# Attention in a transformer layer: softmax weights left unnormalised, row sums from a column of ones, division after the context's reload

## The reference

```python
q, k, v = (split_heads(x @ w + b) for w, b in ((wq, bq), (wk, bk), (wv, bv)))
scores = einsum('bhqd,bhkd->bhqk', q, k) * 48 ** -0.5 + attn_bias[:, None]
attn = softmax(scores, axis=-1)
ctx = einsum('bhij,bhjd->bhid', attn, v)          # back to (b, n, 384)
x1 = rmsnorm(x + ctx @ wo + bo, alpha1, gamma1)
x2 = rmsnorm(x1 + silu(x1 @ w1 + b1) @ w2 + b2, alpha2, gamma2)
out = layernorm(x + x2)
```

## Time and profile before

| | us |
|---|---|
| median of 3 runs | 2019.77 |
| lowest, highest | 2019.53, 2022.11 |
| profiled execution, its own time | 2022.79 |
| its span, first to last instruction | 2021.0 |
| busy: PE, PEld, DVE, ACT, POOL | 1951.2, 1696.9, 1457.0, 1231.1, 1007.5 |
| mean granted TensorE clock | 0.990 |

### The profile page before, as it was taken

The page is one execution under the profiler, slowest core; times in us unless marked ns, Lnnn a source line. Parts: engine busy times, 40 slices in busy tenths (PEclk is TensorE's granted clock), DMA queues, the critical chain, the costliest instruction groups (busy, mean ns, idle before and its releaser), DMA issues. The chain is left out here.

```text
span 2021.0 us, 37267 instructions
## 1 busy us (share of the span) xinstructions
PE 1951.2 (97%) x10336; PEld 1696.9 (84%) x10336; DVE 1457.0 (72%) x3022; ACT 1231.1 (61%) x2408; POOL 1007.5 (50%) x1005
## 2 busy tenths in 40 slices
PE   6999999999999999999996999999999999999998
PEld 5887878888788878888775899999999999999997
DVE  5898899888898898988994555655555555555644
ACT  4887788877887788878874444444433443444332
POOL 3444444443444444443453666555556665555643
PEclk8999999999999999999997999999999999999999
DMA  6444544456444544456434222222111222222011
GB/s 204 117 125 121 164 125 128 125 139 164 110 124 125 159 130 134 119 137 164 111 89 157 83 75 78 78 78 78 66 55 43 72 76 78 78 78 78 16 40 39
DMA packets 114581, 210.12 MB, mean 104 GB/s; under 512 B 18160, under 2 KB 46576, under 8 KB 114544
## 3 DMA queue, kind: packets, MB, share of 16 engines
q1 hardware_dynamic: 114544, 209.67, 35.6%
HBM read 96.35 MB, written 37.75 MB: 66 GB/s over the span
## 5 line engine op out<-in xcount | busy, mean ns | idle before, releaser
L376 POOL TENSOR_SCALAR probs<-probs,inv_sum 128x512 f32<-128x512 f32 x256 | 401.9, 1570 | 515.7 <-DVE inv_sum L545 514.2
L444 ACT ACTIVATE probs<-probs,neg_max 128x512 f32<-128x512 f32 x512 | 364.6, 715 | 79.6 <-DVE neg_max L539 79.1
L531 DVE CUSTOM_DVE_ANT_0 probs<-ps_s,adj_s 128x512 f32<-128x512 f32 x480 | 309.6, 681 | 46.1 <-DMA adj_s<-in_adj 42.2
L557 DVE TENSOR_TENSOR pT_lo<-ps_t,pT_hi 128x1024 fp32r<-128x1024 f32 x256 | 312.0, 1219 | 27.5 <-ACT pT_hi L452 26.7
L452 ACT ACTIVATE pT_hi<-ps_t 128x1024 fp32r<-128x1024 f32 x256 | 261.4, 1021 | 88.7 <-PE ps_t L674 86.5
L1132 DVE TENSOR_TENSOR h_lo<-hidden,h_hi 128x512 fp32r<-128x512 f32 x192 | 168.5, 879 | 172.5 <-ACT h_hi L1038 172.0
L674 PEld LDWEIGHTS ps_t<-ident,probs 128*128 128x128 f32 x2048 | 240.2, 141 | 36.3 <-DVE probs L551 2.4
L674 PE MATMUL ps_t<-ident,probs 128*128 128x128 f32 x2048 | 266.8, 273 | 1.5 <-DVE probs L551 1.5
L1247 PE MATMUL ps_y<-w_hi,h_hi 128*128 128x384 f32 x768 | 257.9, 336 | 0.0
L1247 PE MATMUL ps_y<-w_hi,h_lo 128*128 128x384 f32 x768 | 256.6, 334 | 0.0
L1247 PE MATMUL ps_y<-w_lo,h_hi 128*128 128x384 f32 x768 | 256.6, 334 | 0.0
(11 more groups left out here) (104 smaller groups left out, 4071.4 us busy)
## 6 DMA issues: line engine op xcount, KB each, us to landing
q_both<-stage_q SPq DMA_DIRECT2D x192, 192.0 KB, 3.7
ctx_dram<-ctx_stage SPq DMA_DIRECT2D x256, 96.0 KB, 2.0
k_hl<-stage_k SPq DMA_DIRECT2D x192, 96.0 KB, 2.4
adj_s<-in_adj SPq DMA_DIRECT2D x32, 512.0 KB, 3.9
xT_raw<-in_xT SPq DMA_DIRECT2D x16, 768.0 KB, 4.8
ctx_a<-ctx_dram SPq DMA_DIRECT2D x16, 768.0 KB, 4.6
ctx_b<-ctx_dram SPq DMA_DIRECT2D x16, 768.0 KB, 6.1
x<-in_x SPq DMA_DIRECT2D x16, 768.0 KB, 6.5
```

Source lines behind the costliest of these rows:

```text
L376: pool.tensor_scalar(probs[:, at, :], probs[:, at, :], inv_sum[:, at:at + 1], None, ALU.mult).then_inc(probs_ready[1], 1)
L444: nc.scalar.activation(probs[:, at, :], probs[:, at, :], ACT.Exp, bias=neg_max[:, at:at + 1], accum_out=row_sum[:, at:at + 1])\
L531: nc.vector.tensor_tensor_reduce(out=probs[:, at, :], in0=ps_s[qt % 2][:, :], in1=rows, scale=1.0, scalar=-BIG, op0=ALU.add, op1=ALU.max, ...
L557: nc.vector.tensor_tensor(pT_lo[:, h % 2, s, :, :].rearrange("p q k i -> p (q k i)"), ps_t[pair][:, :, :].rearrange("p q n -> p (q n)"), p ...
```

## The change

- `normalise`, `invert_sum` and `negate_max` go, on DVE and POOL alike; so do `row_max`, `row_sum` and the sum in the exponent. The logits instruction computes negated logits and their minimum, which is the bias of the exponent; the exponent has `scale=-1.0` and waits for the logits' own semaphore, tile by tile. The transposes wait for the exponents.
- Columns 48 to 63 of `v_s` hold ones instead of zeros, so rows 48 to 63 of the context's 112 rows are the row sums, 16 equal copies of each.
- `stage_context` copies without bias. One DMA stores all 112 rows. `ctx_dram` is laid out as 128 partitions (16 rows of each of the 8 heads) by 7 parts: 3 of the high half, 1 of the sums, 3 of the low half. The rows of `wo` and the entries of `bv` are permuted on the host to match.
- In the second phase one DMA loads the 7 parts of a batch. DVE inverts the sums (`invert_sums`, one reciprocal of 128 x 512 for each batch), POOL adds the halves and then multiplies by the inverse (`divide_context`, three more instructions of 128 x 512). `bv` is loaded first in SP's queue and added in `context_high` and `context_low`.
- The inversion for batch 0 stands in DVE's step 6 of the last attention batch, that for batch 1 behind `h_lo` of tile 1 of the first feed-forward batch, the others behind the first `second_residual` of each batch.

```diff
+        self.ctx_raw = sb("ctx_raw", [P, CTX_PARTS, N])
+        self.inv_sum = sb("inv_sum", [P, N])
...
     def load_context(self, sp, ctx_dram, b):
-        for part, buf in enumerate((self.ctx_a, self.ctx_b)):
-            sp.dma_start(buf[:, :, :], ctx_dram[b, part].rearrange("(k p) n -> p k n", p=P))\
-              .then_inc(self.ctx_loaded, DMA)
+        sp.dma_start(self.ctx_raw[:, :, :], ctx_dram[b]).then_inc(self.ctx_loaded, DMA)
+
+    def invert_sums(self, nc, dve, b):
+        dve.wait_ge(self.ctx_loaded, DMA * (b + 1))
+        wait_past(dve, self.ctx_divided, KT * b)
+        nc.vector.reciprocal(self.inv_sum[:, :], self.ctx_raw[:, KT, :]).then_inc(self.sum_inverted, 1)
+
+    def divide_context(self, pool, b):
+        pool.wait_ge(self.ctx_loaded, DMA * (b + 1))
         for k in range(KT):
-            pool.tensor_tensor(self.ctx_a[:, k, :], self.ctx_a[:, k, :], self.ctx_b[:, k, :], ALU.add)\
-                .then_inc(self.ctx_summed, 1)
+            pool.tensor_tensor(self.ctx_raw[:, k, :], self.ctx_raw[:, k, :], self.ctx_raw[:, KT + 1 + k, :], ALU.add)\
+                .then_inc(self.ctx_added, 1)
+        pool.wait_ge(self.sum_inverted, b + 1)
+        for k in range(KT):
+            pool.wait_ge(self.ctx_added, KT * b + k + 1)
+            pool.tensor_tensor(self.ctx_raw[:, k, :], self.ctx_raw[:, k, :], self.inv_sum[:, :], ALU.mult)\
+                .then_inc(self.ctx_divided, 1)
...
             def store_context(b, h):
-                for part, row in enumerate((0, LO)):
-                    sp.dma_start(ctx_dram[b, part, h * DH:(h + 1) * DH, :],
-                                 ctx_stage[row:row + DH, h % 2, :]).then_inc(ctx_stored[h % 2], DMA)
+                sp.dma_start(ctx_dram[b, h * ROWS:(h + 1) * ROWS, :, :].rearrange("r k n -> k r n"),
+                             ctx_stage[0:V_COLS, h % 2, :]).then_inc(ctx_stored[h % 2], DMA)
...
-            pool.memset(v_s[:, :, :, DH:LO].bitcast(FP32), 0.0).then_inc(consts_ready, 1)
+            pool.memset(v_s[:, :, :, DH:LO].bitcast(FP32), 1.0).then_inc(consts_ready, 1)
...
             def exponent(b, h, qt):
-                act.wait_ge(neg_max_ready, pair_no(b, h, qt // 2))
-                nc.scalar.activation(probs[:, at, :], probs[:, at, :], ACT.Exp,
-                                     bias=neg_max[:, at:at + 1], accum_out=row_sum[:, at:at + 1])\
-                  .then_inc(exp_done, 1)
+                wait_apart(act, logits_ready, score_no(b, h, qt), consts_ready)
+                nc.scalar.activation(probs[:, at, :], probs[:, at, :], ACT.Exp, scale=-1.0,
+                                     bias=neg_max[:, at:at + 1]).then_inc(exp_done, 1)
...
                     nc.vector.tensor_tensor_reduce(out=probs[:, at, :], in0=ps_s[qt % 2][:, :],
-                                                   in1=rows, scale=1.0, scalar=-BIG,
-                                                   op0=ALU.add, op1=ALU.max,
-                                                   accum_out=row_max[:, at:at + 1]).then_inc(logits_ready, 1)
+                                                   in1=rows, scale=-1.0, scalar=BIG,
+                                                   op0=ALU.add, op1=ALU.min,
+                                                   accum_out=neg_max[:, at:at + 1]).then_inc(logits_ready, 1)
...
             def transpose_probs(b, h, pair):
-                for i in range(2):
-                    pe.wait_ge(probs_ready[i], pair_no(b, h, pair))
+                pe.wait_ge(exp_done, score_no(b, h, 2 * pair + 1))
...
+            sp.dma_start(bv_c[:, :], bvT).then_inc(bv_loaded, DMA)
             load_x1_rows(0)
...
-                nc.scalar.activation(ctx_hi[:, k, :], ctx_a[:, k, :], ACT.Copy).then_inc(ctx_hi_done, 1)
+                nc.scalar.activation(ctx_hi[:, k, :], ctx_raw[:, k, :], ACT.Identity,
+                                     bias=bv_c[:, k:k + 1]).then_inc(ctx_hi_done, 1)
```

More of the change, by code:

```diff
@@ L54 @@
 V_COLS = LO + DH
+ROWS = 16
+assert H * ROWS == P and DH == KT * ROWS and LO == DH + ROWS
+CTX_PARTS = V_COLS // ROWS
 STACK_DMAS = [2 * len(heads_of_tile(t)) for t in range(KT)]
@@ L289, in stack_projection @@
                 if not isinstance(earlier, int) or earlier >= 0:
-                    wait_apart(sp, scores_ready, score_no(earlier, heads_of_tile(t)[-1], TT - 1), zeroed)
-                wait_apart(sp, proj_lo, proj_no(b, kind, t), zeroed)
+                    wait_apart(sp, scores_ready, score_no(earlier, heads_of_tile(t)[-1], TT - 1), consts_loaded)
+                wait_apart(sp, proj_lo, proj_no(b, kind, t), consts_loaded)
                 sp.wait_ge(proj_hi, proj_hi_no(b, kind, t, len(PARTS_HI[kind])))
@@ L326, in batch @@
                         for par in range(2):
-                            sp.wait_ge(ctx_stored[par], 2 * DMA * H // 2)
+                            sp.wait_ge(ctx_stored[par], DMA * H // 2)
                         shared.load_context(sp, ctx_dram, 0)
@@ L360, in _ @@
             for par in range(2):
-                sp.wait_ge(ctx_stored[par], 2 * DMA * B * H // 2)
+                sp.wait_ge(ctx_stored[par], DMA * B * H // 2)
         @block.gpsimd
@@ L482, in _ @@
                 xT_high(0, k)
-            act.wait_ge(consts_loaded, 3 * DMA)
+            act.wait_ge(consts_loaded, 2 * DMA)
             act.wait_ge(consts_ready, 3)
@@ L560, in pT_low, with batch @@
                                         ALU.subtract).then_inc(pT_lo_done, 1)
-            def batch(b):
+            def batch(b, last=False):
                 for p in range(PAIRS):
@@ L565, in batch @@
                         logits(*ahead)
-                    for pair in pairs_of(b, p + AHEAD - 1):
-                        invert_sum(*pair)
-                    for ahead in pairs_of(b, p + AHEAD):
-                        negate_max(*ahead)
                     for step, kind, t in steps_of(p - 1, b, "qk"):
@@ L572, in batch @@
                     pT_low(b, p // 2, p % 2)
-                    for pair in pairs_of(b, p + AHEAD - 1):
-                        normalise(*pair)
+                    if p == 6 and last:
+                        shared.invert_sums(nc, dve, 0)
                     for _, _, kt in steps_of(p, b, "v"):
@@ L593, in _ @@
                 if n == "k":
-                    dve.wait_ge(consts_loaded, 3 * DMA)
+                    dve.wait_ge(consts_loaded, 2 * DMA)
                     nc.vector.tensor_scalar(bq_c[:, :], bq_c[:, :], DH ** -0.5, None, ALU.mult)\
@@ L614, in _ @@
                 batch(b)
-            batch(LAST)
+            batch(LAST, last=True)
         @block.tensor
@@ L1054, in batch @@
                                 context_high(b + 2, k)
+            act.wait_ge(bv_loaded, DMA)
             for k in range(KT):
@@ L1140, in batch @@
                         finish(b - 1, TT - 1)
+                    if first and j == 1:
+                        shared.invert_sums(nc, dve, 1)
                     if first and j in CTX_AT:
@@ L1152, in batch @@
                     second_residual(b, t)
+                    if t == 0 and two_more:
+                        shared.invert_sums(nc, dve, b + 2)
                     if t >= 1:
@@ L1162, in batch @@
                             context_low(b + 2, k)
+            dve.wait_ge(bv_loaded, DMA)
             for k in range(KT):
@@ L1264, in _, with transformer_layer @@
             batch(LAST, two_more=False, last=True)
[L1267 removed]
+def transformer_layer(nc, x, xT, adj, wq, bqT, wk, bkT, wv, bvT, wo, bo, w1, b1T, w2, b2,
                       alpha1, gamma1, alpha2, gamma2, out):
[L1270 removed]
+    ctx_dram = nc.dram_tensor("ctx_dram", (B, P, CTX_PARTS, N), FP32, kind="Internal").ap()
     with ExitStack() as stack:
         shared = Shared(nc, stack)
[L1273 to L1274 removed]
+        attention_phase(nc, shared, xT, adj, wq, bqT, wk, bkT, wv, wo, ctx_dram)
+        feed_forward_phase(nc, shared, x, ctx_dram, bvT, bo, w1, b1T, w2, b2, alpha1, gamma1, alpha2, gamma2, out)
 def kernel(x, adj, **layer):
```

92 lines of the change are left out of this document (27 added, 65 removed).

## The result

The change makes the kernel slower: 2065.93 us (median of 4 runs, 2053.79 to 2078.08) against 2019.65, a ratio of 1.023 [1.0206, 1.0254]. 1989 was forecast. The profiled execution took 2066.02 us, its span is 2064.2, 43.2 more than before.

What follows compares the result with a forecast made beforehand. PE was taken to set the pace, losing 2.34 us an attention batch to pauses. Terms: -29.1 (15 batches) - 5.1 (last batch) + 0.5 (reciprocal) + 2.5 (transition) = -31.2 us from 2019.8, so 1989 us, range 1978 to 2004.

Steps and rivals of the forecast that it cites:

- the `adj` wait: First phase: PE's 0.99 us pause behind the late `adj` load; issued some 1.0 us earlier, 0.2 to 0.5 us stays.
- Rival 2: The single seven-group store costs as much as two or lands late; the `adj` wait stays whole: 2002 us, chance 0.15.
- all of the 2.34 us as given back: First phase: PE loses 2.34 us a batch to pauses; all returns except 0.4 us, a gain of 1.94 us.
- The floor: First phase: PE's steps in a batch without waiting sum to 62.35 us, against 64.69 us taken.
- of 0.1 to 0.3 us in steps where DVE is behind: First phase: PE's pauses other than the largest, put down to DVE falling behind, which the change would end.
- The reciprocal: Last attention batch, DVE's step 6: new reciprocal taken at 0.70 us, upper bound 4.46, of which 0.5 us reaches PE.
- The last batch's double step: Last attention batch, bound by DVE: two steps go from 6.48 to 5.55 us, a gain of 5.1 us.
- The transition: Start of the second phase: `bv` load 0.41 us, reciprocal and POOL's multiplications 2.1 us; 2.5 us more.
- DVE's and POOL's busy time: First phase, window of 400 us: DVE busy near 270 us, POOL near 25.
- rival 5: Negated logits might take two passes, 1.36 us for 0.68, making DVE the bound: 2100 us, chance 0.04.
- the second phase's steady state: Feed-forward batches: POOL's extra 3.8 us is covered by 9.3 us of slack; costs nothing, 57.3 us a batch.
- Rival 4: PE is already the bound and nothing comes back: 2020 us or 2 more, chance 0.05.

Runs made afterwards that it cites:

- run 2: Changed kernel with a 112-row context store, DRAM rows reordered to (part, row, head) so the load stays one DMA: 2016.07 us, ratio 0.998.
- run 5: Changed kernel with the softmax statistics (maximum, sums, reciprocal, both normalisations, waits) put back, rearranged store and later division kept: 2069.09 us, ratio 1.0245.
- run 6: Changed kernel, rearranged store kept, with each batch's second `adj` load issued ahead of the store, amid the q1 stacking: 1991.96 us, ratio 0.9859.
- run 12: Run 2's store layout plus run 6's early `adj` load, and the first feed-forward batch's reciprocal one step earlier: 1986.8 us, ratio 0.9842.
- run 7: Kernel before, with only the second `adj` load moved into the q1 stacking and nothing of the change: 1995.08 us, ratio 0.9876.
- run 1: Changed kernel with a plain 112-row context store, the rearrangement moved to the second phase's load, in eight loads: 2103.62 us, ratio 1.0406.

## Why the prediction was wrong

**The step that failed** is the `adj` wait. The prediction said: "one of two stores out of the queue, 0.43 us", the landing as before, so that "of the pause [...] 0.2 to 0.5 us stays". The lower bound for the store ("nothing, if one DMA of 112 rows costs what two of 48 did") came out, at 0.88 us for 0.85; the landing had no bound at all. It was held at 4.47 us and became 6.46, because the transfer in front of it changed its shape (runs 2 and 5). The 1 us of an earlier issue came to 0.6: from the start of q's projection it is 12.50 us to the load's issue (621.43 to 633.93), and it was 13.12 (597.96 to 611.08). That is less than the 2 us lost.

**Rival 2 had the mechanism** ("the single store with its rows in seven groups [...] lands late") with a chance of 0.15, and priced it at 2002 us, since it capped the pause at today's 1.3 us. A transfer that lands later than now makes a longer pause than now: with the measured 65.3 us for a batch, 15 x 0.65 = 10 us more than before instead of 16 less. And a second effect had no place in the forecast: behind a longer pause PE runs at half clock. It is the larger part, up to 32 of the 46 us (68.3 - 3.4, halved). The kernel before stood just short of it: its pauses were 1.1 to 1.7 us, but one of 2.2 that had a drop behind it.

**The gain was in large part put down to the wrong cause.** The prediction took "all of the 2.34 us as given back, except for the `adj` wait". It gave that wait 1.3 us of them, of which 0.4 stay, and DVE's falling behind the other 1.0. The floor was right to 0.1 us (62.35; runs 6 and 12 have 62.3 to 62.4), but by run 7 the wait's share is 1.8 us, and 0.5 are DVE's. Run 7 gets 25 of the 28 us without touching DVE. The pauses "of 0.1 to 0.3 us in steps where DVE is behind" were counted as DVE's own; by run 7 about half of them went with the `adj` wait. The change as such is worth some 3 us (run 6 against 7, 1991.96 and 1995.08, with intervals that overlap, so it is not clear of noise). The profiles agree on the size: 10.0 us less in the 15 batches, 0.6 less in the last one, 1.6 more at the handover and 5.2 more behind it. They also show run 6 entering its first batch 2.8 us later, which kernels without the change do too (41.5 to 44.3 us), so that is left out.

**The reciprocal** was mis-sized: 0.70 us taken, 3.34 measured, the upper bound 4.46. The last batch's double step came as forecast (5.46 us for 5.55, 998.40 less 992.94 in run 6), but DVE's reciprocal there stops PE, 0.5 us in the sum and this in the same run (DVE, then PE):

```profile
1001.67 3.34 DVE L167 RECIPROCAL inv_sum<-ctx_raw 128x512 f32<-128x512 f32 x1
...
1005.62 0.73 PE L629 MATMUL ps_s<-k_hl,q_both 96*128 96x512 f32 x1 [2.25 <-DVE neg_max L524]
```

With the half clock behind that pause the last batch gained 0.6 us against run 7's, not 4.6; in run 12, without the drop, 1.8. The Trainium skill's rule, that the prediction weighed and left out of the sum (an estimated 4.3 us), was nearer to the measured 3.34 us than the row of two elements with its 0.70.

**The transition** cost 5.7 us for 2.5. The chain of waits, and POOL beside it, of the changed kernel:

```profile
1144.99 3.26 DVE inv_sum L167
1148.80 2.76 DVE w_lo L1048
```

```profile
1148.33 6.08 POOL L177 TENSOR_TENSOR ctx_raw<-ctx_raw,inv_sum 128x512 f32<-128x512 f32 x3 [4.49 <-DVE inv_sum L167]
```

The reciprocal stands on the chain with nearly its whole length, and while POOL multiplies (2.03 us each for 1.27), DVE's `w_lo` takes 2.76 us for 1.76.

**What was right**: DVE's and POOL's busy time, logits at one pass (rival 5 out), unpaused steps of 3.65 and 3.86 to 3.89 us, and the second phase's steady state: PE 600 of 600 us, and the whole 5.7 us lie at its start. Rival 4, PE as the bound already, is out in both directions: the change lost 46 us, and run 7 gained 25.

## What to carry to other kernels

When a transfer changes shape, look at what is issued behind it, and bound the landing of that, not only the issue. Here a rearrangement with 7 parts outermost cost 50 us that the same bytes in 112 rows did not. Before work is taken off an engine that "falls behind", move the wait that it is behind for; here the place of one load in a queue was worth 25 us and the rewritten softmax some 3. A pause has a second price if it is long enough for the clock to fall behind it, so an edit that lengthens one from 1.4 to 3 us costs more than the difference, and one that shortens it can give more.

## What the runs showed of the hardware

- A granted clock of half the level for 3.4 to 6.8 us behind PE pauses of 1.8 us and more, never behind the 41 shorter ones, always behind the 25 over 3.5 (the table above).
- A store whose outermost dimension is 7 takes 0.88 us of SP's queue where the same bytes in 112 rows take 0.36, and the load behind it lands 1.4 us later by the median (5.9 and 4.5). With nothing beside it, SP waits 4.60 us from its issue on, and 2.71 for the same bytes in 112 rows.
- A reciprocal of 128 x 512 in fp32 takes DVE 3.34 us.
- Eight loads of 16 partitions each land in 9.1 us with the DMA engines 89% busy at 131 GB/s (window 1350 to 1370 of run 1), where one load of all partitions lands in 7.9. Which part of that is theirs was not tested.
